# A gated cross-attention block with a mixture of experts on one core: the small work of the gate and of the second layer norm divided anew over VectorE, GpSimd and ScalarE, and the splitting of two expert weights moved from VectorE to GpSimd

## The reference

```python
x = x + tanh(g_xattn[0]) * xattn(layernorm(x), ctx, Wq1, Wk1, Wv1, Wk2, Wv2, Wo, bo)
x = x + tanh(g_ffn[0]) * ffn(layernorm(x), gate_w, gate_b, w1, b1, w2, b2, ws1, bs1, ws2, bs2)

# xattn: 8 heads of 64; keys and values are the 256 own rows and the 512 context rows;
#        softmax(q k^T / 8) v, then @ Wo + bo
# ffn:
logits = xf @ gate_w + gate_b                 # 512 rows, 8 experts
top_w, top_i = top_k(logits, 2)
gw = softmax(top_w)
combine = (gw[:, :, None] * one_hot(top_i, 8)).sum(axis=1)
for e in range(8):
    h = gelu(xf @ w1[e] + b1[e])              # 128 -> 512
    out = out + combine[:, e:e+1] * (h @ w2[e] + b2[e])
out = out + gelu(xf @ ws1 + bs1) @ ws2 + bs2  # a ninth, shared expert
```

## Time and profile before

| | |
|---|---|
| time, median of 3 runs | 174.17 us (174.34, 174.17, 173.14) |
| profiled execution | 173.16 us, of which the span of the core is 171.0 us |
| mean granted TensorE clock | 0.95 |
| TensorE busy | 144.5 us, 84% of the span |
| VectorE | 128.6 us, 75% |
| GpSimd | 123.9 us, 72% |
| ScalarE | 119.3 us, 70% |
| the chain that ended last | TensorE 40%, VectorE 30%, DMA 8%, GpSimd 6%, ScalarE 3% |

### The profile page before, as it was taken

One profiled execution on the slowest core, in us unless ns is written; L12 is line 12 of the kernel. 1 busy time (PEld: TensorE's weight loads), 2 busy tenths in 40 slices (PEclk: granted clock), 3 DMA queues, 4 the chain that ended last, 5 costly groups with the idle time before them and its releaser, 6 DMA issues.

```text
span 171.0 us, 4386 instructions
## 1 busy us (share of the span) xinstructions
PE 144.5 (84%) x1724; PEld 113.6 (66%) x1724; DVE 128.6 (75%) x267; ACT 119.3 (70%) x200; POOL 123.9 (72%) x98
## 2 busy tenths in 40 slices
PE   7789788568799989989997984999993599999973
PEld 4545334334578778767775873889992389999972
DVE  2779998647668868768698699877899955668681
ACT  3469663408989979889989896585964068787740
POOL 7639999619999999986879794836759355984430
PEclk9999999858999999999999997899999579999999
DMA  5599899970004701984000043000000000000002
GB/s 140 173 341 223 216 216 248 230 204 2 4 2 96 186 0 27 220 262 143 4 0 4 0 126 122 1 4 2 6 0 0 4 0 0 4 0 4 0 0 65
DMA packets 12925, 14.00 MB, mean 82 GB/s; under 512 B 1469, under 2 KB 9578, under 8 KB 12906
## 3 DMA queue, kind: packets, MB, share of 16 engines
q1 hardware_dynamic: 12906, 13.73, 30.4%
HBM read 7.18 MB, written 0.26 MB: 43 GB/s over the span
## 4 chain that ended last, share of the span: by engine, by line
PE 40%; DVE 30%; DMA 8%; POOL 6%; SPq 6%; issue 4%; ACT 3%; ACTq 0%; DVEq 0%
PE banks L951 8%; PE banks L952 8%; PE banks L953 8%; DVE nmax L783 4%; DVE v_lo L768 3%; DMA kab<-k_nat 3%; DMA ring<-in_L_ffn_w_dram 3%; PE banks L1051 2%; PE banks L1052 2%; SPq L452 2%; DVE wf L937 2%; PE banks L1032 2%; POOL p_lo L548 2%; DMA prob<-in_ctx_dram 2%; DVE kab L898 2%
## 5 line engine op out<-in xcount | busy, mean ns | idle before, releaser
L548 POOL TENSOR_TENSOR p_lo<-prob,p_hi 128x768 f16<-128x768 f32 x31 | 51.1, 1667 | 5.0 <-ACT p_hi L649 4.5
L783 DVE TENSOR_REDUCE nmax<-banks 128x1 f32<-128x768 f32 x32 | 30.5, 953 | 13.0 <-PE banks L1033 13.0
L587 POOL TENSOR_TENSOR kab<-kab 128x512 f16<-128x512 f32 x18 | 20.7, 1156 | 17.7 <-ACT kab L696 17.7
L641 ACT ACTIVATE prob<-banks 128x768 f32<-128x768 f32 x32 | 25.8, 805 | 9.1 <-PE banks L1052 8.1
L649 ACT ACTIVATE p_hi<-prob 128x768 f16<-128x768 f32 x32 | 27.0, 843 | 1.0
L690 ACT ACTIVATE kab<-banks,b1T 128x256 f32<-128x256 f32 x36 | 15.1, 471 | 17.5 <-PE banks L953 15.4
L951 PE MATMUL banks<-wf,kab 128*128 128x128 f16 x144 | 25.6, 222 | 1.0 <-DVE acc L929 0.9
L952 PE MATMUL banks<-wf,kab 128*128 128x128 f16 x144 | 25.6, 222 | 0.0
L953 PE MATMUL banks<-wf,kab 128*128 128x128 f16 x144 | 25.5, 222 | 0.0
L1052 PE MATMUL banks<-qab,kab 66*128 66x256 f16 x96 | 23.6, 278 | 0.0
L1051 PE MATMUL banks<-qab,kab 128*128 128x256 f16 x96 | 23.6, 278 | 0.0
(11 more groups left out here) (148 smaller groups left out, 392.1 us busy)
## 6 DMA issues: line engine op xcount, KB each, us to landing
ring<-in_L_ffn_w_dram SPq DMA_DIRECT2D x16, 256.0 KB, 3.9
kab<-k_nat SPq DMA_DIRECT2D x4, 384.0 KB, 4.6
kab<-k_nat SPq DMA_DIRECT2D x6, 192.0 KB, 4.5
kab<-k_nat SPq DMA_DIRECT2D x2, 576.0 KB, 7.1
qab<-qo SPq DMA_DIRECT2D x2, 384.0 KB, 6.3
kab<-k_nat SPq DMA_DIRECT2D x2, 288.0 KB, 8.0
prob<-in_ctx_dram SPq DMA_DIRECT2D x2, 256.0 KB, 4.7
ring<-in_L_xattn_Wk_dram SPq DMA_DIRECT2D x2, 256.0 KB, 4.2
```

What stands on the lines that cost most here:

```text
L548: nc.gpsimd.tensor_tensor(p_lo[:, j % 3, dst, :], prob(j, g)[:, 0:n, :], p_hi[:, j % 3, dst, :], ALU.subtract).then_inc(pl_done, 1)
L783: nc.vector.tensor_reduce(nmax[:, i, q:q + 1], span(0, KEYS), AX_X, ALU.max, negate=True).then_inc(max_done, 1)
```

## The change

Four things are done, with no effect on what is computed.

- The lo parts of experts 3 and 4 leave VectorE (L937 goes). GpSimd does all six late experts with a scaling and a subtraction: expert 3 both at step 18, expert 4 at steps 19 and 20, expert 5 at 21 and 22 (before: 19 and 20), expert 6 at 24 and 25, expert 7 at 27 and 28, expert 8 at 30 and 31. ScalarE's high parts of experts 5 to 8 come one step later.
- The second layer norm: VectorE keeps the statistics. GpSimd adds epsilon, takes the power, and works out minus mean and minus mean by inverse root (four instructions in a chain for each sequence, before one). ScalarE applies scale and bias (`normal_rows`, two instructions for each sequence) at step 15 between the two halves of a head, and at the start of step 22.
- The gate: VectorE adds the bias, takes the maxima and marks the two chosen logits, and later sums and inverts (2 instructions). GpSimd does, in a chain of four, logit minus the greatest, e to that for all 8 experts of both tiles (128 x 16, before 128 x 2), the mask, and the product. ScalarE makes the combine weights (`combine`, 3 instructions) at the end of steps 18 and 25, after that step's GELUs.
- VectorE's lo part of the last head (`last_lo`) moves from the middle of step 18 to its front, and VectorE waits for `comb_ready` only in front of the first weighted sum of a sequence.

```diff
-LO_BY_DVE = [3, 4]
-HI_STEP = {3: 13, 4: 14, 5: FFN0, 6: FFN0 + 3, 7: FFN0 + 6, 8: FFN0 + 9}
-LO_STEP = {3: 16, 4: 17, 5: FFN0 + 1, 6: FFN0 + 5, 7: FFN0 + 8, 8: FFN0 + 11}
+HI_STEP = {3: 13, 4: 14, 5: FFN0 + 1, 6: FFN0 + 4, 7: FFN0 + 7, 8: FFN0 + 10}
+SCALE_STEP = {3: FFN0, 4: FFN0 + 1, 5: FFN0 + 3, 6: FFN0 + 6, 7: FFN0 + 9, 8: FFN0 + 12}
+LO_STEP = {3: FFN0, 4: FFN0 + 2, 5: FFN0 + 4, 6: FFN0 + 7, 7: FFN0 + 10, 8: FFN0 + 13}
...
                 elif j >= RING + EARLY:
-                    sp.wait_ge(f_lo_dve, LO_BY_DVE.index(j - RING) + 1)
+                    sp.wait_ge(f_lo, j - RING - EARLY + 1)
...
-                pool.wait_ge(f_scaled, j - EARLY + 1 - len(LO_BY_DVE))
+                pool.wait_ge(f_scaled, j - EARLY + 1)
                 hi, lo = [wf[:, a, EORDER[j], :, :].rearrange("p a n -> p (a n)") for a in range(2)]
                 nc.gpsimd.tensor_tensor(lo, ring_f(j).rearrange("p a n -> p (a n)"), hi,
-                                        ALU.subtract).then_inc(f_lo_pool, 1)
+                                        ALU.subtract).then_inc(f_lo, 1)
...
                     if s == TAIL_WO:
                         t = NT + QT * b
                         pool.wait_ge(var_ready, 2 + b)
-                        nc.gpsimd.tensor_tensor(rstd[:, t:t + QT], vare[:, t:t + QT], c_mhalf[:, t:t + QT],
-                                                ALU.pow).then_inc(rstd_ready, 1)
+                        link(nc.gpsimd.tensor_scalar(vare[:, t:t + QT], mv[:, t:t + QT, 1], EPS, None, ALU.add))
+                        link(nc.gpsimd.tensor_tensor(rstd[:, t:t + QT], vare[:, t:t + QT], c_mhalf[:, t:t + QT],
+                                                     ALU.pow))
+                        at = slice(QT * b, QT * b + QT)
+                        link(nc.gpsimd.tensor_scalar(away[:, 0, at], mv[:, t:t + QT, 0], -1.0, None, ALU.mult))
+                        nc.gpsimd.tensor_tensor(away[:, 1, at], away[:, 0, at], rstd[:, t:t + QT],
+                                                ALU.mult).then_inc(rstd_ready, 1)
                     if s == TAIL_GATE:
-                        pool.wait_ge(gexp_go, b + 1)
-                        nc.gpsimd.tensor_tensor(gexp[:, QT * b:QT * b + QT], c_e[:, :],
-                                                gdiff[:, QT * b:QT * b + QT], ALU.pow).then_inc(gexp_done, 1)
+                        at = slice(QT * b, QT * b + QT)
+                        pool.wait_ge(pick_done, b + 1)
+                        link(nc.gpsimd.tensor_tensor(gap[:, at, :], logit[:, at, 0:E],
+                                                     top8[:, at, 0:1].broadcast_to([P, QT, E]), ALU.subtract))
+                        link(nc.gpsimd.tensor_tensor(gap[:, at, :], c_e[:, :].unsqueeze(2).broadcast_to([P, QT, E]),
+                                                     gap[:, at, :], ALU.pow))
+                        link(nc.gpsimd.tensor_scalar(mask[:, at, :], marked[:, at, 0:E], PICKED, None, ALU.is_equal))
+                        nc.gpsimd.tensor_tensor(first[:, at, :], gap[:, at, :], mask[:, at, :],
+                                                ALU.mult).then_inc(gate_done, 1)
                 k = i - FFN0 - 1
                 if 0 <= k < NF:
                     pool.wait_ge(hh_act, k + 1)
                     nc.gpsimd.tensor_tensor(hid_lo[:, k % HB, 0:HALF], hid_a[:, k % 2, :], hid_hi[:, k % HB, 0:HALF],
                                             ALU.subtract).then_inc(hl_pool, 1)
                 for j in range(EARLY, NE):
-                    if j not in LO_BY_DVE and i == LO_STEP[j]:
+                    if i == SCALE_STEP[j]:
                         scale_late(j)
-                    if j not in LO_BY_DVE and i == LO_STEP[j] + 1:
+                    if i == LO_STEP[j]:
                         lo_late(j)
...
+            def normal_rows(b):
+
+                act.wait_ge(rstd_ready, 2 + b)
+                for t in range(QT * b, QT * b + QT):
+                    nc.scalar.activation(xn[:, t, :], acc[:, t, :], ACT.Identity, bias=away[:, 1, t:t + 1],
+                                         scale=rstd[:, NT + t:NT + t + 1]).then_inc(xn_ready, 1)
+
+            def combine(b):
+
+                act.wait_ge(gate_sum, b + 1)
+                tiles = slice(QT * b, QT * b + QT)
+                for t in range(QT * b, QT * b + QT):
+                    nc.scalar.activation(comb[:, t, 0:E], first[:, t, :], ACT.Identity,
+                                         scale=gtop[:, t, 0:1]).then_inc(comb_part, 1)
+                act.wait_ge(comb_part, QT * (b + 1))
+                nc.scalar.activation(comb_s[:, tiles, :], comb[:, tiles, :], ACT.Identity,
+                                     scale=scales[:, 1:2]).then_inc(comb_ready, 1)
+
             for i in range(STEPS):
+                if i == TAIL_STEP[1][TAIL_X]:
+                    normal_rows(1)
...
+                if i == TAIL_STEP[0][TAIL_X]:
+                    normal_rows(0)
...
+                for b in range(B):
+                    if i == TAIL_STEP[b][TAIL_COMB]:
+                        combine(b)
...
-                    mark(nc.vector.bn_aggr(mv[:, first + t, :], stats[:, first + t, :]))
+                    last = nc.vector.bn_aggr(mv[:, first + t, :], stats[:, first + t, :])
+                    if first > 0 and t == tiles - 1:
+                        last.then_inc(var_ready, 1)
+                    else:
+                        mark(last)
                 settle()
+                if first > 0:
+                    return
...
                 tiles = slice(QT * b, QT * b + QT)
-                if s == TAIL_X:
-                    normalise_rows(acc[:, tiles, :], NT + QT * b, QT, 2 + b)
                 if s == TAIL_COMB:
 
-                    dve.wait_ge(gexp_done, b + 1)
-                    link(nc.vector.tensor_scalar(gsum[:, tiles], gexp[:, tiles], 1.0, None, ALU.add))
-                    link(nc.vector.reciprocal(gtop[:, tiles, 0], gsum[:, tiles]))
-                    mark(nc.vector.tensor_tensor(gtop[:, tiles, 1], gtop[:, tiles, 0], gexp[:, tiles], ALU.mult))
-                    link(nc.vector.tensor_tensor(first[:, tiles, :], first[:, tiles, :],
-                                                 gtop[:, tiles, 0:1].broadcast_to([P, QT, E]), ALU.mult))
-
-                    link(nc.vector.tensor_tensor(first[:, tiles, :], first[:, tiles, :],
-                                                 gtop[:, tiles, 1:2].broadcast_to([P, QT, E]), ALU.max))
-                    link(nc.vector.tensor_tensor(comb[:, tiles, 0:E], first[:, tiles, :], mask[:, tiles, :],
-                                                 ALU.mult))
-                    nc.vector.tensor_scalar(comb_s[:, tiles, :], comb[:, tiles, :], scales[:, 1:2], None,
-                                            ALU.mult).then_inc(comb_ready, 1)
-                    dve.wait_ge(comb_ready, b + 1)
+                    dve.wait_ge(gate_done, b + 1)
+                    link(nc.vector.tensor_reduce(gsum[:, tiles], first[:, tiles, :], AX_X, ALU.add))
+                    nc.vector.reciprocal(gtop[:, tiles, 0], gsum[:, tiles]).then_inc(gate_sum, 1)
...
-                    mark(nc.vector.tensor_copy(pick8[:, tiles, 0:2], top8[:, tiles, 0:2]))
-                    nc.vector.tensor_tensor(gdiff[:, tiles], top8[:, tiles, 1], top8[:, tiles, 0],
-                                            ALU.subtract).then_inc(gexp_go, 1)
-                    mark(nc.vector.tensor_tensor(first[:, tiles, :], logit[:, tiles, 0:E],
-                                                 top8[:, tiles, 0:1].broadcast_to([P, QT, E]), ALU.is_equal))
-                    settle()
+                    link(nc.vector.tensor_reduce(pick8[:, tiles, 0:2], top8[:, tiles, 0:2].unsqueeze(3), AX_X, ALU.max))
                     for t in range(QT * b, QT * b + QT):
-                        mark(nc.vector.match_replace(marked[:, t, :], pick8[:, t, :], logit[:, t, :], PICKED))
-                    settle()
-                    mark(nc.vector.tensor_scalar(mask[:, tiles, :], marked[:, tiles, 0:E], PICKED, None,
-                                                 ALU.is_equal))
+                        last = nc.vector.match_replace(marked[:, t, :], pick8[:, t, :], logit[:, t, :], PICKED)
+                        if t < QT * b + QT - 1:
+                            mark(last)
+                    last.then_inc(pick_done, 1)
...
             for i in range(STEPS):
+                if i - HI_LAG == LO_LAST:
+                    last_lo(LO_LAST)
...
+                    if k == first_pass(b):
+                        dve.wait_ge(comb_ready, b + 1)
...
-                for j in LO_BY_DVE:
-                    if LO_STEP[j] == i:
-                        dve.wait_ge(f_hi, j - EARLY + 1)
-                        e = EORDER[j]
-                        nc.vector.scalar_tensor_tensor(
-                            out=wf[:, 1, e, :, :].rearrange("p a n -> p (a n)"),
```

(7 more changed lines are left out.)

12 lines of the change are left out of this document (5 added, 7 removed).

## The result

The changed kernel takes 176.82 us (median of 20 runs, 173.92 to 181.95), the kernel before 172.94 us (20 runs, 170.33 to 176.11). The ratio is **1.021 [1.016, 1.026]**, 3.9 us slower. The prediction said 178.2 us in 172 to 180, and slower with 0.60. (The median of the three runs of before that the prediction had lay 1.2 us above that of the 20.)

What follows compares the result with a forecast made beforehand. TensorE's waits for combine weights (7.3 us) and the lowered clock after them (3.3) were taken as the bound. 173.16 plus 5.2 for sequence 1's later COMB gave 178.4, set to 178.2 us for overlapping GpSimd instructions; range 172 to 180.

Steps and rivals of the forecast that it cites:

- likeliest case: The forecast itself, chance 0.50: expert 5's lo part on GpSimd makes pass 5 late; 178.2 us.
- Sequence 0, worth 0: COMB of sequence 0 stays near 105, since ScalarE's order replaces VectorE's delay; gain 0.
- a move of over 1 us: Sign against the forecast: COMB of sequence 0 moving by over 1 us.
- Experts 3 and 4, worth 0: GpSimd finishes both splits at 115.7 to 116.7, before pass 4's first matmul ends near 119.25; cost 0.
- Expert 5, +4.4: GpSimd does its lo part behind sequence 1's layer norm, ending at 125.2; pass 5 starts 4.4 us later.
- The clock behind expert 5, +1.0: TensorE's clock falls after idling for expert 5; pass 5's first product costs 1.0 us more.
- The gate's chain on GpSimd, 4.05: Sequence 1's subtract, power, compare and multiply take 4.05 us, the power on 128x16 being 3.0.
- `hid_lo` and the GELUs queued behind it: Pass 5's `hid_lo`, pass 7's GELUs and `combine` follow the gate chain; sequence 1's COMB at 139.8, +5.2 us in all.
- After COMB, 0: Behind sequence 1's COMB the clock falls again and 2.0 us are lost as before; change 0.
- Rival D: ScalarE's new function needs its own table, loads adding some 8 us on the path, 186 us; chance 0.04.
- Rival B: Sequence 1's gate chain: cheap GpSimd instructions, clock losses avoided, VectorE's 5.9 us gone; 171.9 us, faster; chance 0.18.

Runs made afterwards that it cites:

- e6: Changed kernel with 30 matmuls on zeros, results unread, in front of pass 5's wait for its weights; 175.23 against 173.47 us, ratio 1.007.
- e5: Changed kernel with expert 5's lo part alone done by VectorE at its step 21; 173.29 against 173.47 us, ratio of medians 0.999, too uneven for an interval.
- e8: Changed kernel with expert 5's lo part on VectorE and pass 5's `hid_lo` in front of GpSimd's gate chain; 170.06 against 173.47 us, ratio 0.980.
- e1: Changed kernel with the splits of experts 3, 4 and 5 put back as before; 175.51 against 173.28 us, ratio 1.004.
- e3: Changed kernel with the gate's power on 2 values of a partition instead of 16, output not the reference's; 173.27 against 173.28 us, ratio 1.001.
- e4: Changed kernel with pass 5's `hid_lo` in front of the gate chain on GpSimd instead of behind it; 173.77 against 173.28 us, ratio 0.998.
- e7: Kernel before with 44 matmuls on zeros in front of the wait for COMB of sequence 1; 171.25 against 173.87 us, ratio 0.984.
- e2: Kernel before with only the new split of the late experts, gate and layer norm as before; 182.75 against 173.28 us, ratio 1.052.
- e9: Kernel before with GpSimd's splits of experts 6, 7 and 8 later, clear of VectorE's gate; 168.79 against 173.47 us, ratio 0.973.
- e11: Changed kernel with experts 3, 4 and 5 split as before and pass 5's `hid_lo` in front of GpSimd's gate chain; 171.72 against 173.87 us, ratio 0.991.

## Why the prediction was right, and where a size was off

**Direction and mechanism: right.** Its likeliest case came: GpSimd, which was to relieve VectorE, became the late engine. Point by point:

- *Sequence 0, worth 0.* COMB at 106.61 instead of 105.29, 1.3 us later. The prediction had named a move of over 1 us as a sign that it is wrong. The sign is of no use here: pass 0's first matmul already came 1.3 us late, at 100.64 instead of 99.37, and e6, the same kernel up to that point, had it at 98.23 and COMB at 104.20. The clock was 0.83 from 30 to 50 us in after's execution and 1.00 in e6's. One profiled execution of each cannot settle a move of 1.3 us. The clock held behind COMB this time, so pass 2's first matmul came at 110.97 against 111.07. The release came from ScalarE, as foreseen. The relief of VectorE was worth nothing there.
- *Experts 3 and 4, worth 0.* Nothing waited for them: the one wait for an expert's lo part is pass 5's. GpSimd was through with them at 116.48 (forecast 115.7 to 116.7), 0.3 us before the layer norm's statistics came. The 1.71 us that the prediction took as VectorE's best price for such a split were stretched as well: beside nothing that holds it, one takes 1.22 us (e5).
- *Expert 5, +4.4.* Measured +3.9. The layer norm's chain took 1.6 us instead of 1.75, the scaling 1.90 instead of 2.07, the rest as summed. The wait was 3.39 us. e8, without this work on GpSimd and with the clock held behind COMB of sequence 0 as in after, has A 3.2 us shorter. e5 and e1 show only 1.9 and 2.0 us, with the clock down there.
- *The clock behind expert 5, +1.0.* It fell to 0.61, and the last mark came 6.26 us after pass 5's start (forecast 6.6, before 5.77). e6 keeps it up at this place: 0.9 us less in B, 1.4% in the time.
- *The gate's chain on GpSimd, 4.05.* Measured 131.04 to 134.91, 3.87; the power 2.91 against 3.0. The straight line through 0.70 and 1.03 us held at four times the size. e3 has it shorter by 2.2 us, of which 1.65 us show in COMB of sequence 1; the time falls by 2%, more than that.
- *`hid_lo` and the GELUs queued behind it.* As forecast, and e4 shows the queue: with nothing but the order changed, B falls by 2.9 us. COMB of sequence 1 stood at +4.45 us; the sum had +5.2.
- *After COMB, 0.* **This term was mis-sized.** From COMB of sequence 1 to the end of the span it was 34.6 us, 1.75 less than before (36.4), because the clock stayed at 1.00 behind it. I had given TensorE idle pieces of 2.5 and 1.5 us there; they were 2.54 and 1.47, and this time they did not bring the clock down. In e1, e5 and e6, where pass 5 is in time or kept warm, the first piece was 3.36, 3.25 and 3.32 us, and the clock was down at or behind this COMB. e7 shows what the lower level costs at this place: 2.1 us to pass 9, 2.7 in the time. With this term the sum is 178.4 - 0.75 - 1.75 = 175.9, against 175.5 measured. That the other executions of after, up to 181.95, are those in which the clock fell at more places is only argued, since one execution was profiled; their mean clocks (0.924 in the longest, 0.979 in the shortest) go that way, though not every one does (0.990 at 176.26 us).
- *Rival D* did not come: after has two table loads (L643 and L723, 1.28 us each), as before has.

**Two questions that the prediction left out.** It took the stretched instructions as a property of VectorE's share and asked what moving them would cost. e2 and e9 show that they are GpSimd's doing. And it took the two halves of the change as a sum, which they are not: the new split alone is 1.052, the new division alone 1.004, both together 1.021. The divided layer norm was never run apart from the divided gate, so what each of them gives is not known. With the gate still on VectorE, a GpSimd without idle time stretches all of it, for sequence 0 to 8.6 us (100.82 to 109.44). So the division saves 3% once the split has been moved, and nothing without that, as long as `hid_lo` stands behind the gate; with that mended as well it saves 0.9% without the moved split (e11).

Rival B (faster) had the right reason, that the 5.9 us go, and failed on the power's 2.91 us and on expert 5. Two faults of order did most of the harm, expert 5 behind the layer norm and `hid_lo` behind the gate, and neither belongs to the idea: e8 mends both and is 2% faster than before, with the 2.91 us power still in it. e9 gets at least as much, 2.7%, for three numbers (the two intervals overlap).

## What to carry to other kernels

When small instructions of one engine come out ten times as long as their twins, add start and length and see with whose instruction they end, before you move them: keeping that neighbour away may be the whole remedy (e9). Moving work onto an engine with idle time moves it into a list, so look at what stands behind the waiting instruction there (e4) and at what now finishes last in that list (e1, e5). Parts of a change can have opposite signs and depend on each other; only the runs with each part alone showed it. And where one execution is profiled, see where its clock fell before you compare two lengths in it.
